# A four-layer gated block on one core: a projection's squares moved to VectorE, a bias moved to GpSimd, shorter routers, and a mixing loop turned one pair ahead

## The reference, cut to what matters

```python
x = x + tanh(g_xattn[0]) * causal_attention(_layernorm(x), ctx, ctx)        # 16 heads
x = x + tanh(g_ffn[0])   * quantised_swiglu(_layernorm(x), ...)
x = x + tanh(g_xattn[1]) * layernorm(z + mean_of_decayed_scan(ctx)) * gamma + beta
x = x + tanh(g_ffn[1])   * (einsum(z, factors).sum_over_r / sqrt(8) + bias)  # "mixing"
x = x + tanh(g_xattn[2]) * where(any(mask), softmax(where(mask, z @ ctx.T / 16, -1e30)) @ ctx, 0)
x = x + tanh(g_ffn[2])   * moe(z)      # 8 experts, the best 2 of 8 sigmoid scores, one shared expert
x = x + tanh(g_xattn[3]) * (attention(rms_norm(z @ w_q.T + b_q, g_q), k_img, v_img) @ w_o.T + b_o)
x = x + tanh(g_ffn[3])   * moe(z)      # 7 experts, best 2 of 7 logits + bias, one shared expert
```

## Time and profile before

| what | value |
|---|---|
| runs of the kernel, three | 903.51 us median, 902.8 to 904.79 |
| the profiled execution | 905.36 us, with a span of 903.5 us |
| granted clock of TensorE over the span | 0.909 of full speed |
| busy: PE, DVE, ACT, POOL | 762.5, 589.0, 420.9, 341.4 us |
| PE's share of the chain that ended last | 53% |

### The profile page before, as it was taken

The page is one execution under the profiler, slowest core; times in us unless marked ns, Lnnn a source line. Parts: engine busy times, 40 slices in busy tenths (PEclk is TensorE's granted clock), DMA queues, the critical chain, the costliest instruction groups (busy, mean ns, idle before and its releaser), DMA issues.

```text
span 903.5 us, 16057 instructions
## 1 busy us (share of the span) xinstructions
PE 762.5 (84%) x4547; PEld 503.1 (56%) x4555; DVE 589.0 (65%) x1388; ACT 420.9 (47%) x920; POOL 341.4 (38%) x571
## 2 busy tenths in 40 slices
PE   3999896998684289898999968999997889999982
PEld 2455454555342156595788756566666555666641
DVE  5799696778776966874322382688874865444446
ACT  3566464676571013341377557666662233333320
POOL 5000552455347613337367652000020761333320
PEclk9999897999997597957999989899997799999995
DMA  6354309999008890144445362000004222232226
GB/s 207 121 175 126 99 9 301 310 287 312 22 0 323 304 283 1 42 183 143 143 147 152 105 195 86 20 20 21 12 1 140 94 95 77 84 87 86 66 79 215
DMA packets 90507, 116.86 MB, mean 129 GB/s; under 512 B 12421, under 2 KB 81064, under 8 KB 89146
## 3 DMA queue, kind: packets, MB, share of 16 engines
q1 hardware_dynamic: 83658, 99.01, 36.2%
q0 software_dynamic: 6768, 16.86, 5.2%
HBM read 54.90 MB, written 58.43 MB: 125 GB/s over the span
## 4 chain that ended last, share of the span: by engine, by line
PE 53%; DVE 14%; SPq 9%; issue 8%; ACT 8%; POOL 5%; DMA 3%; DVEq 0%; POOLq 0%; ACTq 0%
PE ps L2195 8%; SPq L398 7%; PE ps L2086 5%; PE ps L1770 5%; PE ps L2217 4%; POOL x_rows L601 3%; PE ps L1760 3%; PE ps L2104 3%; ACT work L824 2%; ACT probs_t L830 2%; PE ps L1966 2%; PE ps L2079 2%; PE ps L1806 2%; PE ps L2162 2%; PE ps L2069 2%
## 5 line engine op out<-in xcount | busy, mean ns | idle before, releaser
L830 ACT ACTIVATE probs_t<-ps 128x1024 f32<-128x1024 f32 x64 | 65.6, 1024 | 72.8 <-PE ps L1770 72.8
L1223 DVE TENSOR_REDUCE row_max<-ps 128x8 f32<-128x1024 f32 x64 | 77.5, 1210 | 12.0 <-PE ps L1760 11.8
L1087 ACT ACTIVATE ctx_cols<-ctx_cols 128x256 f32<-128x256 f32 x54 | 22.5, 417 | 124.0 <-DVE ctx_cols L1619 124.0
L1229 DVE TENSOR_TENSOR work<-ps,row_max 128x1024 f32<-128x1024 f32 x64 | 76.9, 1202 | 1.2
L1619 DVE TENSOR_TENSOR ctx_cols<-ps,ctx_rows 128x512 f32<-128x512 f32 x54 | 37.3, 690 | 60.6 <-PE ps L2195 60.5
L1770 PE MATMUL ps<-ident,work 128*128 128x128 f32 x512 | 70.6, 282 | 3.3 <-ACT work L824 2.1
L2195 PE MATMUL ps<-early,xt 128*128 x152 | 71.5, 593 | 0.0
L2217 PE MATMUL ps<-early,ctx_cols 128*128 (+1 forms) x216 | 57.7, 391 | 12.2 <-ACT ctx_cols L1092 12.2
L1770 PEld LDWEIGHTS ps<-ident,work 128*128 128x128 f32 x512 | 57.2, 143 | 18.7 <-ACT work L824 13.2
L642 POOL DMA_INDIRECT y_rows<-ctx_cols,w2d x38 | 37.5, 988 | 78.7 <-DMA y_rows<-ctx_cols,w2d 49.0
L2217 PEld LDWEIGHTS ps<-early,ctx_cols 128*128 128x128 f32 x216 | 41.7, 195 | 41.5 <-issue 23.2
(11 more groups left out here) (328 smaller groups left out, 1895.7 us busy)
## 6 DMA issues: line engine op xcount, KB each, us to landing
x_rows<-pad_row SPq DMA_DIRECT2D x1, 17415.0 KB, 68.5
work<-x_rows SPq DMA_DIRECT2D x77, 129.0 KB, 2.1
x_rows<-pad_row SPq DMA_DIRECT2D x1, 7740.0 KB, 36.0
x_rows<-pad_row SPq DMA_DIRECT2D x1, 7611.0 KB, 93.7
early<-in_w3st SPq DMA_DIRECT2D x8, 512.0 KB, 6.4
work<-y_rows SPq DMA_DIRECT2D x16, 256.0 KB, 2.9
early<-y_rows SPq DMA_DIRECT2D x8, 512.0 KB, 7.4
late<-in_w2u SPq DMA_DIRECT2D x1, 2304.0 KB, 8.7
```

Source lines behind the costliest of these rows:

```text
L830: act.activation(probs_t[:, :, :], ps[:, 4:6, :], ACT.Copy).then_inc(sem("att.evac"), 1)
L1223: dve.tensor_reduce(row_max[:, u, 8 * c:8 * c + 8], scores(c), AX.X, ALU.max).then_inc(sem("att.max"), 1)
L1229: dve.tensor_tensor(probs[:, u, c, :].rearrange("p (h k) -> p h k", k=P), scores(c), row_max[:, u, 8 * c:8 * c + 8].unsqueeze(2).to_broadc ...
```

## The change

It has five parts.

1. **Squares.** `q_sq` is made by DVE from the evacuated queries in `xt_all`, 16 of ACT's instructions becoming 8 of DVE's, placed between the `take_back2` of later pairs. It has four buffers for two, and PE's sums run one pair later.
2. **Output bias.** PE's bias matmul in `project_out` goes. SP loads `b_o` to all partitions, POOL multiplies it by the gate once and adds it to the 16 tiles of `x` after it has staged the values of a pair. DVE's addition of a tile waits for it.
3. **Routers.** `route` uses one comparison, its product with a triangular mask, the difference from its own transpose, and a sum over the row: 4 instructions for 6. The count is then shifted by a constant for each expert, so that the mask and the one-hot rows compare with rows of constants (`offset`), and the two one-hot instructions become one.
4. **Mixing.** PE transposes pair `t + 2` ahead of multiplying pair `t`, with two buffers `xt4`; the loop is written out, and DVE normalises two pairs ahead.
5. **One-head attention.** ACT's evacuation multiplies by -1/16, so that the scores come out negated and the row minimum is at once the bias of the exponential; L1450 goes (16 instructions), and the mask has the other sign.

```diff
@@ mixing, ACT @@
-            tile_pairs(act, front_ring(3))
+            for k in range(NT // 2):
+                for u in range(2):
+                    act.wait_ge(sem("front.tr"), FRONT[3] + 2 * k + u + 1)
+                    wait(act, sem("main3"), 2 * k + u - 3)
+                    act.activation(xt4[k % 2][:, u], bank(TP + u, D).rearrange("p (j n) -> p j n", j=2),
+                                   ACT.Copy).then_inc(sem("front.out"), 1)
@@ mixing, DVE @@
             norm_x(3, 0)
+            norm_x(3, 2)
+            for t in range(0, NT, 2):
+                if t + 4 < NT:
+                    norm_x(3, t + 4)
                 for u in range(2):
                     dve.wait_ge(sem("main3"), t + u + 1)
                     add_gated(3, t + u, bank(4 + u, D), tg[:, 5:6])
@@ mixing, PE @@
+            turn_mix(0)
+            for t in range(0, NT, 2):
+                if t + 2 < NT:
+                    turn_mix(t + 2)
+                mixing(t)
@@ one-head attention, DVE @@
-                    dve.tensor_reduce(sc_l2[:, u, 0:1], bank(u, P), AX.X, ALU.max).then_inc(sem("l2.max"), 1)
-                for u in range(2):
-                    dve.wait_ge(sem("l2.max"), 2 * k + u + 1)
-                    dve.tensor_scalar(sc_l2[:, u, 1:2], sc_l2[:, u, 0:1], -(D ** -0.5), None, ALU.mult
-                                      ).then_inc(sem("l2.bias"), 1)
+                    dve.tensor_reduce(sc_l2[:, u, 1:2], bank(u, P), AX.X, ALU.min).then_inc(sem("l2.least"), 1)
@@ route and choose, DVE @@
-                dve.tensor_tensor(ra, sj, se, ALU.is_ge).then_inc(sem("dve.self"), 1)
-                ns[0] += 1
-                seq(dve.tensor_tensor(rb, sj, se, ALU.is_gt))
-                seq(dve.tensor_tensor(ra, ra, rb, ALU.subtract))
+                seq(dve.tensor_tensor(ra, sj, se, ALU.is_ge))
                 seq(dve.tensor_tensor(ra, ra, lo, ALU.mult))
-                seq(dve.tensor_tensor(ra, ra, rb, ALU.add))
-                seq(dve.tensor_reduce(place, ra, AX.X, ALU.add))
+                seq(dve.tensor_tensor(rb, ra, ra.rearrange("p t e j -> p t j e"), ALU.subtract))
+                seq(dve.tensor_reduce(place, rb, AX.X, ALU.add))
...
-                for k in range(2):
-                    seq(dve.tensor_scalar(oh[:, k, q], cnt[:, q], float(k), None, ALU.is_equal))
+                seq(dve.tensor_tensor(oh[:, :, q], cnt[:, q].unsqueeze(1).to_broadcast([P, 2, 4, E]),
+                                      offset[:, :, o:8].unsqueeze(2).to_broadcast([P, 2, 4, E]), ALU.is_equal))
@@ query projection, DVE @@
+            def query_squares(t):
+                q = xt_all[:, :, t * P:(t + 2) * P]
+                upto(dve, "qkv.out", t + 2)
+                if t >= 8:
+                    upto(dve, "qkv.sum", t - 6)
+                dve.tensor_tensor(q_sq[:, t // 2 % 4], q, q, ALU.mult).then_inc(sem("qkv.sq"), 2)
+
             take_back2(0)
...
             for t in range(2, NT, 2):
                 take_back2(t)
+                if t >= 8:
+                    query_squares(t - 8)
+            for t in range(NT - 8, NT, 2):
+                query_squares(t)
@@ query projection, PE @@
-                if t:
-                    query_sums(t - 2)
+                if t >= 4:
+                    query_sums(t - 4)
+            for t in range(NT - 4, NT - 2, 2):
+                query_sums(t)
@@ output bias, SP, POOL, DVE, PE @@
+            sp.dma_start(bo_rows, a["bo"]).then_inc(sem("load.w3x"), 16)
...
+            TT(bo_rows, bo_rows, tg[:, 3:4].to_broadcast([P, D]), ALU.mult).then_inc(sem("qk.gain"), 1)
+            for t in range(0, NT, 2):
+                stage_values(3, t)
+                if t == 0:
+                    pool.wait_ge(sem("xn"), 7 * NT)
+                    pool.wait_ge(sem("qk.gain"), 2)
+                for u in range(2):
+                    TT(x[:, t + u, :], x[:, t + u, :], bo_rows, ALU.add).then_inc(sem("out3.bias"), 1)
...
                         dve.wait_ge(sem("out3.proj"), t + 1)
+                        upto(dve, "out3.bias", t + 1)
                         add_gated(6, t, bank(7, 2 * D, D), tg[:, 3:4])
...
-                    mm(bank(7, 2 * D, D), ones3[32:35, :], b_o, start=True, stop=False)
```

More of the change, by code:

```diff
@@ L223, in build @@
         mask_bf = rows_bf[0:1, 0:NT * P].rearrange("p (t n) -> p t n", t=NT)
-        b_mix, b_kv, b_o = (bias3[:, i * D:j * D] for i, j in ((0, 1), (2, 4), (4, 5)))
+        b_mix, b_kv = (bias3[:, i * D:j * D] for i, j in ((0, 1), (2, 4)))
         valid = sb("valid", [P, NT])
@@ L801, in _ @@
             pool.wait_ge(sem("stage.zero"), 2)
-            tile_pairs(pool, lambda t, first, last: stage_values(3, t))
+            pool.wait_ge(sem("load.w3x"), 16 * 3)
+            TT(bo_rows, bo_rows, tg[:, 3:4].to_broadcast([P, D]), ALU.mult).then_inc(sem("qk.gain"), 1)
[6 more added lines that the diff above has]
+                    TT(x[:, t + u, :], x[:, t + u, :], bo_rows, ALU.add).then_inc(sem("out3.bias"), 1)
             deviations(7)
@@ L956, in exp_l2 @@
                 for u in range(2):
-                    act.wait_ge(sem("l2.bias"), 2 * k + u + 1)
+                    act.wait_ge(sem("l2.least"), 2 * k + u + 1)
                     wait(act, sem("l2.tr"), 2 * k + u - 1)
-                    act.activation(p_l2[:, u], bank(u, P), ACT.Exp, scale=D ** -0.5, bias=sc_l2[:, u, 1:2],
+                    act.activation(p_l2[:, u], bank(u, P), ACT.Exp, scale=-1.0, bias=sc_l2[:, u, 1:2],
                                    accum_out=sc_l2[:, u, 2:3]).then_inc(sem("l2.exped"), 1)
@@ L966, in rows_l2 @@
                     act.activation(xt4[k % 2][:, u], bank(TP + u, D).rearrange("p (j n) -> p j n", j=2),
-                                   ACT.Copy).then_inc(sem("front.out"), 1)
+                                   ACT.Copy, scale=-(D ** -0.5)).then_inc(sem("front.out"), 1)
             for k in range(NT // 2 + 2):
@@ L1053, in query_out @@
                 op.then_inc(sem("qkv.out"), 2)
-                if t >= 4:
-                    upto(act, "qkv.sum", t - 2)
-                for j in range(2):
-                    op = act.activation(q_sq[:, t // 2 % 2, j], bank(2 + t // 2 % 2, (j + 1) * 2 * P, j * 2 * P), ACT.Square,
-                                        bias=bq_c[:, j:j + 1])
-                op.then_inc(sem("qkv.sq"), 2)
             norm6(0)
@@ L1420, in _ @@
             norm_x(3, 0)
-            def mixing(t, first, last):
-                if not last:
-                    norm_x(3, t + 2)
+            norm_x(3, 2)
+            for t in range(0, NT, 2):
+                if t + 4 < NT:
+                    norm_x(3, t + 4)
                 for u in range(2):
@@ L1427, in mixing @@
                     add_gated(3, t + u, bank(4 + u, D), tg[:, 5:6])
-                if last:
+                if t + 2 == NT:
                     norm_x(4, 0)
                 tile_stats(4, t, sem("resid3"))
-            for t in range(0, NT, 2):
-                mixing(t, t == 0, t == NT - 2)
             def weights_l2(k):
@@ L1956, in _, with turn_mix, mixing @@
             pe.wait_ge(sem("kv.out"), NT)
-            def mixing(t, first, last):
+            def turn_mix(t):
                 for u in range(2):
                     front(3, t + u, u, lambda u: pe.wait_ge(sem("qf.y"), NT))
+            def mixing(t):
                 for u in range(2):
@@ L2170, in query_sums @@
                     for j in range(2):
-                        op = mm(ps[:, 4, t + u:t + u + 1], q_sq[:, t // 2 % 2, j, u * P:(u + 1) * P], ones8[:, 0:1], start=(j == 0),
+                        op = mm(ps[:, 4, t + u:t + u + 1], q_sq[:, t // 2 % 4, j, u * P:(u + 1) * P], ones8[:, 0:1], start=(j == 0),
                                 stop=(j == 1))
```

39 lines of the change are left out of this document (17 added, 22 removed).

## The result

The changed kernel takes 895.88 us (median of 4 runs, 894.69 to 896.32); the kernel before, run beside it, 904.15. The ratio is 0.9909, with a 95% interval of 0.9885 to 0.9933: 8.3 us less, of 8.2 forecast.

The account below looks back on a forecast made before the run. PE was taken to bound most of the span, with DVE bounding the one-head attention. The terms -2.4 - 1.7 - 0.8 + 0 - 3.3 + 0 = -8.2 took 903.5 to 895.3 us, range 892.5 to 899.3.

Parts of the forecast that it names:

- a move of the sends by another amount than 4.1: Sign of a wrong prediction: POOL's first send was to come 4.1 us earlier, by what the stages ahead gave.
- Mixing, -2.4: Mixing loop: a pair falls from 3.45 to 3.06, 3.1 over eight, less 0.3 at the start and 0.4 for waits.
- One-head attention, -1.7: One-head attention: DVE loses L1450, 0.20 in each of seven passes plus the loop's ends; 1.7 us less.
- rival C: First slot after the sends: PE's new wait of 1.5 lowers its clock, costing about 3.5; 898.8 us, chance 16%.
- Router 1, -0.8: First router to first slot: sends keep POOL's pace, PE gains only the 0.74 it was late; 0.8 us less.
- Rival B: First slot: PE's whole lead passes, its 1.5 wait gained too; sign a PE shift over 6; 893.8 us, chance 14%.
- Rival D: Query projection: DVE gets late with the squares and PE's pair grows, costing 2.5; 897.8 us, chance 12%.
- Rivals G and N: G: mixing gains nothing, 897.7 us, 6%. N: mixing and one-head attention gain nothing, 903.7 us, 3%.
- Projection, 0: Query projection: a pair stays 3.04, all PE, with DVE's squares covered by its lead; 0, ends -0.3 and +0.3.
- Output bias, -3.3: 16-head attention: PE loses the bias matmul L1804, 0.21 a tile in 16 tiles; 3.3 us less.
- Rival E: 16-head attention: POOL's sixteen additions of 0.72 hold DVE, 11.5 unhidden; 906.8 us, slower, chance 5%.
- Router 2, 0: Second router: POOL's sends keep their own pace, so DVE's four shorter groups pass on 0, up to 0.4.

Follow-up runs that it names:

- only_mixing: The kernel before with only the mixing part of the change; ratio 0.9965 to the kernel before.
- all_but_squares: The changed kernel with the squares back on ACT and PE's sums one pair behind, as before; ratio 0.9914 to the kernel before.
- early_rms: The changed kernel with the query norms made in two halves, the first during the projection; ratio 0.9883 to the kernel before.
- warm: The changed kernel with unread transposes on idle PE before mixing, at the seam after it, before the first router and at the projection's start; ratio 0.9826 to the kernel before.
- best: The changed kernel with unread transposes (none before the router), query norms in halves and later sums; 886.76 us, ratio 0.9835 to the kernel before.
- only_routers: The kernel before with only the routers part of the change; ratio 0.9978 to the kernel before.
- seam_filled: The kernel before with twelve unread transposes on PE at the seam between mixing and one-head attention; ratio 0.9988 to the kernel before.
- only_one_head: The kernel before with only the one-head attention part of the change; ratio 1.0000 to the kernel before.
- all_but_mixing: The changed kernel with the mixing loop of before and one transpose buffer; ratio 0.9951 to the kernel before.
- only_bias: The kernel before with only the output bias part of the change; ratio 0.9972 to the kernel before.

## Why the prediction was right, and where its terms were not

Mixing, the one-head attention and the output bias gained by the mechanism forecast, router 1 by this and by something more. That the total came out within 0.1 is luck in part: two misses, 0.7 in router 1 and 0.9 in the projection, nearly cancel. And one of the two signs of being wrong that the prediction named did come, a move of the sends by another amount than 4.1. In the profiled pair the first send moved by 6.6 (395.14 to 388.57). What it had wrong there is not the pace of the sends but the clock ahead of them, as the next two paragraphs show.

*Mixing, -2.4: the mechanism as forecast, the profiled pair 1.0 short.* A pair is 2.98. Over the traces the stage took 29.8 to 30.2 with the old loop (eight traces) and 27.2 to 28.5 with the new one (`only_mixing`, the changed kernel, `all_but_squares`, `early_rms`; `warm` and `best` have added work), 2.1 less on average. For the profiled pair the step that was too small is "I charge 0.3 there": the start runs at 1.2 GHz, and in the profiled pair the clock rose 9.1 after PE's first transpose instead of 5.7. That isn't the new loop's own: in its four traces the rise came after 9.0 and 9.1 (28.4 and 28.5) and after 6.5 and 6.9 (27.2 and 27.5). With the old loop it came after 5.6 to 7.3. So at a like rise (30.1 with the old loop) the new one is worth 2.6 to 2.9, no less than forecast. `best` shows what the start costs: with the clock up from the beginning 24.74.

*One-head attention, -1.7: the edit is worth 1.3 to 1.6, and the rest of the 4.9 isn't its own.* The lengths fall into four groups:

```
one-head attention, us      clock falls in full           clock does not fall
code of before              36.03 36.03 36.01 36.02       32.65 32.65
code of the change          34.70 34.66                   31.09 31.07 31.08 31.10
```

Down a column is the edit, 1.3 to 1.6; along a row is the clock, 3.4 to 3.6. (`only_routers` with 33.64 and `all_but_squares` with 32.05 had a fall of some 3 us.) The step that failed is one that I didn't take: the earlier trace rows were read as the price of a fall that the change might bring, in rival C, and not as one that the kernel had and could lose.

*Does the change take the fall away?* With the old loop and nothing in the gaps it came in six of seven traces, in five of them in full; with the new one in two of four, in one of them in full. With transposes in the gaps it came in none of three (`seam_filled`, `warm`, `best`). So with the gaps it came in eight of eleven, and that PE's idle 0.94 and 0.92 at the seam are needed for it is likely, not proven: `only_one_head`, `only_mixing` and the changed kernel have the gaps and no fall, and three filled traces could have missed it too. That the new loop makes it rarer is likely and not shown, and `only_one_head` and `early_rms` are each a case against a simple rule. The Trainium skill, page "TensorE: Matmul & The Clock Gate", section "What's actually happening", says that the window in which activity is looked at runs freely, so that the same work can meet it in different places; the two cases agree with it, and no run here holds the place fixed.

*Router 1, -0.8: right in kind, 1.5 in size.* The 0.74 that PE was late are gone, as worked out, and PE waits. A further 0.6 came from the sends: from the first copy to POOL's first slot 48.41 for 49.01, which I had at nothing. From the first send to slot 0 the traces of the faster chips have 48.4 to 48.9 with the part (five) and 50.0 and 50.3 without (two). Why the sends gained isn't shown. The groups of DVE don't move the first send: with the new code and the clock as before it takes 14.86 to 14.88, for 14.87. The 0.88 in the table are the clock's.

*Rival B.* PE's first weight load at slot 0 moved 7.9, over the 6 that I named as its sign. It is not B: PE waits there, 0.94. The sign was badly chosen, since any gain ahead of the sends moves it too. *Rival C* did not come: behind the wait the clock stayed at 1.00 (435 to 475) in the changed kernel and in `all_but_mixing`, `all_but_squares` and `best`, where PE was idle 0.94, 1.45, 1.22 and 1.56. *Rival D*: DVE waited for ACT's queries, and PE's pair stayed at 3.04. *Rivals G and N* are out by the pair of 2.98 in mixing and by the total.

*Projection, 0: right as a sum, by two terms that I missed.* At the start PE skips a pair of sums and waits 0.62 for ACT instead, so nothing is saved; at the end two pairs stand ahead of the scores, 0.89. The changed kernel gave most of this back by a clock that rose sooner, 7.9 after the stage's first transpose for 9.5.

*Output bias, -3.3: right, 3.1 of its own.* From the first `project_out` to the last are 105.52 to 105.53 in all seven traces without it and 102.36 to 102.40 in all seven with it: 3.1, or 0.21 a tile as forecast, on every chip. From the first scores to the last `project_out` are 123.3 to 123.8 with it (five kernels; `early_rms` and `best` have the early norms besides) and 126.6 to 127.5 without (seven): 3.5 on average. The other 0.4 is in the stage's start, where the clock fell for 3.4 or 6.8 us; in the profiled pair it is 1.0 (the fall was 3.4 for 6.8), and that isn't shown to be the part's. *Rival E* is excluded by DVE's 484 ns.

*Router 2, 0.* The +1.20 and +0.62 of the table can't be given to the change. Of the +1.20, 0.94 is the last `project_out`, whose four products took 2.07 for 1.13 because the clock had just fallen. Over the traces the first of the two stages takes 15.1 to 16.2 without the bias part and 15.4 to 16.3 with it, the second 48.2 to 48.7 without the routers part and 48.3 to 49.2 with it.

By these sizes the sum is -2.1 - 1.5 - 1.5 - 3.5, and 0.9 back in the projection: -7.7 of the 8.3. The rest, and the profiled pair's further 2.3, is less than what the clock at the seam does from trace to trace (0 or 3.5). How often it fell in the runs that were only timed isn't known.

## What to carry to other kernels

Ask of every low clock in the profile of before whether the change could take it away, not only whether it could bring one: here it was worth 3.4 to 3.6 in the stage, more than any edit (3.1 the largest). A stage's cost has a part that its instructions don't show, the stretch after idle time at 1.2 GHz; transposes that nobody reads, put where PE waits, took 3.1 from mixing (24.74 for 27.9 on average), and where they filled the seam its fall of 3.5 did not come, in three traces of three. And name as the sign of a rival something that only the rival does.

## What the runs showed of the hardware

- In the router of `warm`, with its matmuls of 8 columns and transposes, PE was idle at most 0.21 at a time from 370 to 378, and its clock still fell (1.00 at 376, 0.52 at 377, PE busy 1.00 in both). It stayed at 0.50 up to about 400. What made it fall isn't shown.
- Chips 5 and 1 ran the kernel before in 950.7 and 947.9 us; chips 7 and 13 in 904.3 and 903.5. Up to the first send the times are the same but for the clock. From there to slot 0 it took 72 to 78 us for 50: POOL waited for the first slot's transfer 31.14 us in `only_mixing`, and PE stood still for nothing that the profile names (its idle time in this stretch is 21 to 29 us in the traces of these chips, for 5 in the kernel before, at the same number of matmuls), as in this timeline of `only_bias`:

```profile
413.94 0.45 PE L2105 MATMUL ps<-ident,xn 128*128 128x128 f32 x1 [4.09 <-issue]
...
421.30 0.33 PE L2105 MATMUL ps<-ident,xn 128*128 128x128 f32 x1 [2.34 <-issue]
```

  Its cause stays open. It is why the parts that act ahead of the sends may show less in the total there than in the stages.
- The `pow` for 16 columns takes POOL 2.9 us and ACT's table load ahead of the first exponential 1.28. `early_rms` took the wait for the sums out of the way of the first maximum and exponential, which came 1.16 earlier; the rest of its 2.0 is the clock.
